# A layer norm's deviations packed by DMA ahead of the reciprocal, and three steps of the software pipeline placed anew

## The chip, the core and the metric

The kernel runs on one core of one Trainium2 chip. The metric is the device time of one execution in microseconds (us): the median of three runs of the kernel before is 827.21 us.

The engines are named as the profile does: PE (TensorE, matrix products) with PEld (its weight loads), DVE (VectorE), ACT (ScalarE), POOL (GpSimd) and SP (SyncE, which here only issues DMAs; its queue is SPq). Each runs its own instructions in order; they meet through semaphores.

## The reference

The input is x of shape (8, 64, 64, 64): 8 images, 64 channels, 64 x 64 pixels. Two layers follow each other.

Layer 0 runs four scans over the rows and then the columns of the image. Each step adds to a line the relu of a nine-tap convolution (64 to 64 channels) of the line before it: `new = cur + relu(row_conv(prev, K))`.

Layer 1 is a block of a dynamic depthwise convolution, a layer norm, and a pointwise network:

```python
pooled = x.mean((2, 3))
hdn = _ln(pooled @ w_fc1.T, ln1_w, ln1_b, axis=-1)
dyn_w = (hdn @ w_fc2.T).reshape(b * c, 1, K, K)            # K = 5, one 5x5 filter an image and channel
out = depthwise_conv(x, dyn_w)                             # padding 2
u = out.mean(1, keepdims=True)
s2 = jnp.square(out - u).mean(1, keepdims=True)
out = (out - u) * lax.rsqrt(s2 + EPS)                      # over the 64 channels of each pixel
out = ln2_w[None, :, None, None] * out + ln2_b[None, :, None, None]
out = gelu(einsum('bchw,oc->bohw', out, w_expand))         # 64 -> 256 channels, exact gelu
gx = jnp.sqrt(jnp.sum(jnp.square(out), axis=(2, 3), keepdims=True))
nx = gx / (gx.mean(1, keepdims=True) + EPS)
out = gamma * (out * nx) + beta + out
return einsum('bohw,co->bchw', out, w_shrink) + x          # 256 -> 64 channels
```

The change is about the factor `rsqrt(s2 + EPS)`, one number a pixel.

## The kernel before

`scans` computes layer 0 in the first 505 us or so; the change doesn't touch it. `block_two` computes layer 1. Two channels' halves of the image lie on the 128 partitions: partitions 0 to 63 hold the 64 channels of the even rows, 64 to 127 those of the odd rows.

**Units and slots.** The work is cut into 16 units (`UNITS`), two for each image, of 1024 columns each (`UCOLS`). The units pass through a software pipeline of slots, `for s in SLOTS_RUN`, written out by hand for each engine. In slot s

- DVE takes the taps of unit s: ten products (eleven in the units of `EARLY` = 3, 4, 5, 6, 8, 10, 12, 14), each a `scalar_tensor_tensor` into PSUM (L996), and then the addition into `inner` (`add_part`, L981). The first tap waits for PE's convolution of the unit.
- PE makes five other taps of unit s + 1 as 30 products (`conv(0)` to `conv(5)`, L1240, five products each), the statistics of unit w = s - 1 (L1255), four expansions of unit e = s - 2 (L1286) and two shrinking products of unit v = s - 5 (L1312). `conv(0)` waits for the addition into `inner` of unit s - 1.
- ACT squares unit w (L866) and the mean of it (`square_mean`, L871), takes the root (`root`, L877), and makes the four gelus of unit e (L889), squares for the energy (L899) and products for the taps of unit s + 1 (L860). Root and gelu need different activation tables, so a table load of 1.28 us stands ahead of each change.
- POOL normalises unit e (`norm`, L818: `inner` times `rstd_wide`), adds ACT's products (L793), splits x into high and low parts for PE (L783, L788) and in even slots makes the diagonals for the next image (L809).

**The way of a deviation.** `statistics` leaves mean and mean square of unit w in PSUM: in each group of 32 partitions only four rows of 128 columns are meaningful (4 groups x 4 rows x 128 = 2048 numbers, one for each pixel of the unit). `make_var` (L1030, L1032) makes the variance on DVE, ACT's `root` the deviation `std` (128 x 128, L877), `make_rstd` the reciprocal of all 128 x 128 on DVE (L1039). Then SP (`spread_rstd`, L744) stores `rstd` to DRAM (L749) and loads it back twice with a broadcast over 64 partitions each into `rstd_wide` (L756), which POOL's `norm` waits for. The last unit takes another way: PE spreads its reciprocal by products (`widen`, L1260).

**The order around the change.** DVE's order in a slot is: two taps, `finish(v, 0)`, two taps, `sum_energy` (in slots where n = s - 3 is an odd unit), `make_var`, one tap, `make_rstd`, one tap, `finish(v, 1)`, one tap (two in an `EARLY` slot), `respond` (in the same slots as `sum_energy`), and the rest of the taps with the addition. `finish` (L1090) adds the shrunk result to x. `sum_energy` and `respond` (L1065 and L1070 to L1081) turn an image's energies into the factor of the shrinking weights; PE's part of that is `respond` (L1297), which follows `conv(3)`. In the first slots there is no v, and so no `finish` (it begins in slot 5), and no n.

SP runs, slot by slot: `spread_rstd(s - 1)`, `store(s - 5)` (L742, results to DRAM) and `cross(s + 2)` (L733, L735: the other half's rows into `crossed`, after the addition of unit s).

## Time and profile before

| | before |
|---|---|
| median of three runs | 827.21 us (827.14 to 827.62) |
| the profiled execution | 827.7 us, of which the span is 826.0 us |
| PE busy | 776.0 us (94%) |
| PEld busy | 635.3 us (77%) |
| DVE busy | 624.6 us (76%) |
| POOL busy | 450.2 us (55%) |
| ACT busy | 398.9 us (48%) |

A busy share is an average over both layers. The picture in 40 slices of 20.65 us each tells the stages apart: up to slice 24 or so it is layer 0, behind that `block_two`.

```profile
## 2 busy tenths in 40 slices
PE   5999999999999999999999997978899999999886
PEld 5999998999998999999999996644445445454332
DVE  3666666666665666666888887999999999999965
ACT  5591002777774000000000003459989999999981
POOL 2333333333333333335888884988978887888610
PEclk9999999999999999999999996889999999999999
DMA  6670000000000000000000002022233334433234
```

Each digit is the busy share of a slice in tenths; PEclk is the granted clock of TensorE in tenths of full speed, DMA the mean busy share of the 16 DMA engines.

### The profile page before, as it was taken

The page shows a single profiled execution, that of the slowest core. Times are in us where ns is not written, and L with a number is a line of the kernel's source. Part 1 is how long each engine was busy: PE and PEld are TensorE (multiplying, and loading weights), DVE is VectorE, ACT ScalarE, POOL GpSimd, SP SyncE. Part 2 cuts the span into 40 slices and gives each one's busy share as a digit, 9 for nine tenths or more (in the row PEclk, how much of TensorE's full clock was granted, in tenths as well). Part 3 has the DMA queues.
Part 4 walks back from the last instruction along what each step waited for, and adds up shares of the span by engine and source line. Part 5 has one row for each costly group of instructions (what it writes and reads, how often), then busy time and mean ns, then how long its engine had stood idle before and what let it go on. Part 6 is the DMA issues. An engine that isn't in the chain of part 4 may idle for free. (4 is left out here: it accounts for less than half of the span.)

```text
span 826.0 us, 15628 instructions
## 1 busy us (share of the span) xinstructions
PE 776.0 (94%) x5399; PEld 635.3 (77%) x5399; DVE 624.6 (76%) x1143; ACT 398.9 (48%) x491; POOL 450.2 (55%) x450
## 2 busy tenths in 40 slices
PE   5999999999999999999999997978899999999886
PEld 5999998999998999999999996644445445454332
DVE  3666666666665666666888887999999999999965
ACT  5591002777774000000000003459989999999981
POOL 2333333333333333335888884988978887888610
PEclk9999999999999999999999996889999999999999
DMA  6670000000000000000000002022233334433234
GB/s 145 162 179 0 0 0 0 2 0 0 0 0 1 1 0 0 0 0 1 1 0 0 0 0 50 25 64 72 77 81 80 90 92 109 104 79 83 55 77 102
DMA packets 61571, 35.81 MB, mean 43 GB/s; under 512 B 41504, under 2 KB 59488, under 8 KB 61536
## 3 DMA queue, kind: packets, MB, share of 16 engines
q1 hardware_dynamic: 59424, 34.83, 17.8%
q10 hardware_dynamic: 2112, 0.52, 0.3%
q8 instruction: 20, 0.33, 0.2%
q14 instruction: 15, 0.12, 0.0%
HBM read 17.85 MB, written 9.37 MB: 33 GB/s over the span
## 5 line engine op out<-in xcount | busy, mean ns | idle before, releaser
L504 PE MATMUL psum<-line_hi,taps_hi 128*128 128x256 f32 x1270 | 203.0, 292 | 11.8 <-DVE taps_lo L400 8.5
L518 PE MATMUL psum<-line_lo,taps_hi 128*128 128x256 f32 x1270 | 202.5, 291 | 0.8 <-DVE line_lo L453 0.8
L512 PE MATMUL psum<-line_hi,taps_lo 128*128 128x256 f32 x1270 | 202.2, 291 | 0.0
L453 DVE SCALAR_TENSOR_TENSOR line_lo<-psum,rest 128x256 fp32r<-128x256 f32 x254 | 108.0, 425 | 123.9 <-POOL rest L285 114.9
L504 PEld LDWEIGHTS psum<-line_hi,taps_hi 128*128 128x128 f32 x1270 | 177.1, 192 | 13.0 <-issue 9.3
L518 PEld LDWEIGHTS psum<-line_lo,taps_hi 128*128 128x128 f32 x1270 | 176.4, 191 | 1.9 <-DVE line_lo L453 1.7
L512 PEld LDWEIGHTS psum<-line_hi,taps_lo 128*128 128x128 f32 x1270 | 176.9, 191 | 0.0
L285 POOL TENSOR_TENSOR rest<-x,line_hi 128x256 f32<-128x256 f32 x127 | 82.9, 652 | 168.6 <-DVE line_hi L444 168.6
L337 ACT ACTIVATE by_h<-x (+1 forms) x128 | 85.7, 669 | 106.6 <-DVE x L433 105.0
L285 POOL TENSOR_TENSOR rest<-by_h,line_hi 128x256 f32<-128x256 f32 x127 | 91.5, 720 | 83.3 <-DVE line_hi L444 83.3
L793 POOL TENSOR_TENSOR part<-part,prod 128x1008 f32<-128x1008 f32 (+2 forms) x56 | 127.5, 2276 | 17.1 <-ACT prod L860 11.3
L433 DVE TENSOR_TENSOR x<-line_hi,line_lo 128x256 f32 (+1 forms) x190 | 105.6, 556 | 0.2
L996 DVE SCALAR_TENSOR_TENSOR psum<-x,tap_all,psum 128x992 f32<-128x992 f32 (+6 forms) x88 | 103.8, 1180 | 1.4
L996 DVE SCALAR_TENSOR_TENSOR psum<-crossed,tap_cross,psum 128x1008 f32<-128x1008 f32 (+5 forms) x80 | 98.7, 1234 | 2.1 <-PE psum L1240 0.2
L1240 PE MATMUL psum<-x_hi,dyn_hi 128*128 128x512 f32 x160 | 69.0, 431 | 8.3 <-DVE inner L981 4.9
L1286 PE MATMUL psum<-normed,expand_w 64*128 64x512 f32 x224 | 65.1, 661 | 12.3 <-ACT wide L889 12.3
L444 DVE SCALAR_TENSOR_TENSOR line_hi<-psum,x 128x256 fp32r<-128x256 f32 x127 | 53.9, 424 | 22.0 <-PE psum L504 8.6
L1240 PE MATMUL psum<-x_hi,dyn_lo 128*128 128x512 f32 x160 | 68.1, 425 | 0.0
L444 DVE SCALAR_TENSOR_TENSOR line_hi<-psum,by_h 128x256 fp32r<-128x256 f32 x127 | 53.9, 425 | 17.0 <-PE psum L504 3.8
L1240 PE MATMUL psum<-x_lo,dyn_hi 128*128 128x512 f32 x160 | 65.9, 412 | 0.0
L889 ACT ACTIVATE wide<-psum,expand_bias 128x1024 f32<-128x1024 f32 x60 | 65.8, 1103 | 0.3
L293 POOL TENSOR_TENSOR line_sum<-line_sum,x 128x256 f32<-128x256 f32 x63 | 54.8, 870 | 20.2 <-DVE x L433 20.2
(159 smaller groups left out, 760.6 us busy)
## 6 DMA issues: line engine op xcount, KB each, us to landing
stage<-in_x_dram SPq DMA_DIRECT2D x32, 256.0 KB, 4.0
rstd_wide<-rstd_dram SPq DMA_DIRECT2D x30, 256.0 KB, 5.3
out_dram<-x SPq DMA_DIRECT2D x28, 256.0 KB, 5.4
crossed<-x SPq DMA_DIRECT2D x16, 256.0 KB, 3.5
crossed<-x SPq DMA_DIRECT2D x16, 240.0 KB, 3.6
rstd_dram<-rstd SPq DMA_DIRECT2D x15, 64.0 KB, 1.5
out_dram<-x ACTq DMA_DIRECT2D x4, 128.0 KB, 4.7
out_dram<-x SPq DMA_DIRECT2D x4, 128.0 KB, 4.0
```

The costliest lines, as they stand in the source:

```text
L285: pool.tensor_tensor(rest[:, slot % 2, :].rearrange("p (b i) -> p b i", b=B), x_line, line_hi[:, (slot + 1) % SLOTS, :, REACH:REACH + WP]. ...
L337: act.activation(dst, src, ACT.Copy).then_inc(turned, 1)
L433: dve.tensor_tensor(kept_line(s, row_of(s, k)), line_hi[:, made, :, part].bitcast(F32), line_lo[:, made, :, part].bitcast(F32), ALU.add).t ...
L444: dve.scalar_tensor_tensor(out=line_hi[:, (slot + 1) % SLOTS, :, part], in0=as_lines(line_ps[slot][:, 0:LINE]), scalar=0.0, in1=x_line, op ...
L453: dve.scalar_tensor_tensor(out=line_lo[:, (slot + 1) % SLOTS, :, part], in0=as_lines(line_ps[slot][:, 0:LINE]), scalar=0.0, in1=as_lines(r ...
L504: mm = pe.matmul(line_ps[slot][:, 0:LINE], taps_hi[:, s, d, :], line_hi[:, slot, :, d:d + WP], start=(d == 0), stop=(d == OFFSETS - 1))
L512: pe.matmul(line_ps[slot][:, 0:LINE], taps_lo[:, s, d, :], line_hi[:, slot, :, d:d + WP], start=False, stop=False, skip_group_check=True)
L518: mm = pe.matmul(line_ps[slot][:, 0:LINE], taps_hi[:, s, d, :], line_lo[:, slot, :, d:d + WP], start=False, stop=(d == OFFSETS - 1), skip_ ...
L793: pool.tensor_tensor(dst, dst, other, ALU.add).then_inc(part_step, 1)
L889: act.activation(grown(u)[:, m, :, c * COLS:(c + 1) * COLS], exp_set(4 * u + 2 * m + c), ACT.Gelu, bias=expand_bias[:, m:m + 1]).then_inc( ...
L996: dve.scalar_tensor_tensor(out=here, in0=src, scalar=weight, in1=here, op0=ALU.mult, op1=ALU.add).then_inc(tap_step, 1)
L1240: mm = pe.matmul(conv_ps[:, 2 * (u % 2) + c, :], weight[:, b % 2, n, :, :].rearrange("p o c -> p (o c)"), image[:, u % 2, CROWS * c:CROWS ...
```

## The change

It does three things.

1. **Packing.** Four DMAs of SP copy the meaningful rows of `std` (four partitions of 128 columns in each group of 32) into `dense`, 128 partitions of 16 columns. The reciprocal runs on `dense` and is 16 columns wide instead of 128; DVE waits for the four DMAs (`std_dense`) instead of for ACT's root. The store to DRAM takes `dense_rstd` (8 KB instead of 64), and the two loads into `rstd_wide` read the same amount from it in another arrangement. The last unit keeps the wide reciprocal.
2. **DVE's order.** Without `sum_energy` in the slot: two taps, `finish(v, 0)`, one tap, `make_var`, two taps, `finish(v, 1)`, `make_rstd`. With it: two taps, `finish(v, 0)`, two taps, `sum_energy`, `make_var`, two taps, `finish(v, 1)`, `make_rstd`. So the variance moves one tap up in half of the slots, and the reciprocal moves behind `finish(v, 1)`, and in the other half behind one tap more.
3. **PE's order.** `respond` goes ahead of `conv(3)` instead of behind it.

```diff
--- before.py
+++ after.py
@@ -600,6 +600,9 @@
         mean_sq = sb("mean_sq", [P, STAT_COLS])
         var = sb("var", [P, STAT_COLS])
         std = sb("std", [P, STAT_COLS])
+        PER = UCOLS // C
+        dense = sb("dense", [P, PER])
+        dense_rstd = sb("dense_rstd", [P, 2, PER])
         rstd = sb("rstd", [P, 2, STAT_COLS])
         rstd_wide = sb("rstd_wide", [P, UCOLS])
         normed = sb("normed", [P, UCOLS])
@@ -622,7 +625,7 @@
         tap = sb("tap", [P, B, len(PE_TAPS), 2])
         tap_hi = sb("tap_hi", [P, B, len(PE_TAPS), 2], F32R)
         tap_lo = sb("tap_lo", [P, B, len(PE_TAPS), 2], F32R)
-        rstd_dram = nc.dram_tensor("rstd_dram", [2, P, STAT_COLS], F32, kind="Internal").ap()
+        rstd_dram = nc.dram_tensor("rstd_dram", [2, P, PER], F32, kind="Internal").ap()
 
         pads = sem("pads")
         weights_mm = sem("weights_mm")
@@ -653,6 +656,7 @@
         rstd_ready = sem("rstd_ready")
         rstd_stored = [sem(f"rstd_stored{i}") for i in range(2)]
         rstd_spread = sem("rstd_spread")
+        std_dense = sem("std_dense")
         spread_made = sem("spread_made")
         wide_done = sem("wide_done")
         normed_ready = sem("normed_ready")
@@ -743,16 +747,22 @@
 
             def spread_rstd(u):
 
+                sp.wait_ge(std_ready, u + 1)
+                if u > 0:
+                    sp.wait_ge(rstd_ready, u)
+                for g in range(4):
+                    sp.dma_start(dense[32 * g:32 * g + 32, :],
+                                 std[32 * g:32 * g + 2 * SUBS, :].rearrange("q (a n) -> q a n", n=PER)).then_inc(std_dense, 16)
                 sp.wait_ge(rstd_ready, u + 1)
                 if u > 1:
                     sp.wait_ge(rstd_spread, 32 * (u - 1))
-                sp.dma_start(rstd_dram[u % 2], rstd[:, u % 2, :]).then_inc(rstd_stored[u % 2], 16)
+                sp.dma_start(rstd_dram[u % 2], dense_rstd[:, u % 2, :]).then_inc(rstd_stored[u % 2], 16)
                 sp.wait_ge(rstd_stored[u % 2], 16 * (u // 2 + 1))
                 if u > 0:
                     sp.wait_ge(normed_ready, u)
-                rows = rstd_dram[u % 2].rearrange("(g q) n -> g (q n)", g=4)
+                rows = rstd_dram[u % 2].rearrange("(g h q) n -> g h (q n)", g=4, h=2)
                 for h in range(2):
-                    mine = rows[:, SUBS * h * STAT_COLS:SUBS * (h + 1) * STAT_COLS].rearrange("(a g) n -> a g n", a=1)
+                    mine = rows[:, h, :].rearrange("(a g) n -> a g n", a=1)
                     sp.dma_start(rstd_wide[C * h:C * h + C, :].rearrange("p (g n) -> p g n", g=4),
                                  mine.to_broadcast([C, 4, SUBS * STAT_COLS])).then_inc(rstd_spread, 16)
 
@@ -1033,10 +1043,14 @@
                                          op1=ALU.min).then_inc(var_step, 1)
 
             def make_rstd(u):
-                dve.wait_ge(std_ready, u + 1)
                 if u > 1:
                     dve.wait_ge(rstd_stored[u % 2], 16 * (u // 2))
-                dve.reciprocal(rstd[:, u % 2, :], std[:, :]).then_inc(rstd_ready, 1)
+                if u < LAST:
+                    dve.wait_ge(std_dense, 64 * (u + 1))
+                    dve.reciprocal(dense_rstd[:, u % 2, :], dense[:, :]).then_inc(rstd_ready, 1)
+                else:
+                    dve.wait_ge(std_ready, u + 1)
+                    dve.reciprocal(rstd[:, u % 2, :], std[:, :]).then_inc(rstd_ready, 1)
 
             def norm(c):
                 dve.wait_ge(wide_done, c + 1)
@@ -1147,17 +1161,18 @@
                 take(2)
                 if v >= 0:
                     finish(v, 0)
-                take(2)
                 if n in range(UNITS) and n % 2 == 1:
+                    take(2)
                     sum_energy(n // 2)
+                else:
+                    take(1)
                 if w in range(UNITS):
                     make_var(w)
-                take(1)
+                take(2)
+                if v >= 0:
+                    finish(v, 1)
                 if w in range(UNITS):
                     make_rstd(w)
-                take(1)
-                if v >= 0:
-                    finish(v, 1)
                 take(1 + len(dve_taps(s)) - len(DVE_TAPS))
                 if n in range(UNITS) and n % 2 == 1:
                     respond(n // 2)
@@ -1338,9 +1353,9 @@
                 conv(1)
                 conv(2)
                 at_e(0, 1)
-                conv(3)
                 if n in range(UNITS) and n % 2 == 1:
                     respond(n // 2)
+                conv(3)
                 at_e(1, 0)
                 conv(4)
                 conv(5)
```

## Rows read from the trace of the kernel before

**Rows 1.** The waits from 640 to 783 us: engine, line, waited for, total us, times, longest.

```profile
PE psum L1286 <- ACT wide L889: 7.7, 9, 2.7
```

**Rows 2.** The windows of two slots: stretch, its length, busy time of each engine, clock, DMA.

```profile
718.70:738.20 19.50, 19.50 (x110) 9.39 (x106) 18.07 (x24) 19.11 (x21) 15.94 (x9) 1.00 0.39 93
738.20:754.30 16.10, 14.79 (x86) 7.83 (x86) 15.79 (x18) 14.44 (x17) 13.13 (x7) 1.00 0.36 91
```

**Rows 3.** The timeline of DVE, 680 to 752 us: start, duration, operation, idle time before.

```profile
701.38 1.22 DVE L981 SCALAR_TENSOR_TENSOR inner<-part,psum 128x1024 f32<-128x1024 f32 x1
...
721.34 0.75 DVE L1090 SCALAR_TENSOR_TENSOR x<-psum,out_bias,x 128x512 f32<-128x512 f32 x1 [0.18 <-PE psum L1312]
...
724.53 0.28 DVE L1030 TENSOR_TENSOR var<-psum,mean_sq 128x128 f32<-128x128 f32 x1
...
728.68 2.54 DVE L996 SCALAR_TENSOR_TENSOR psum<-x,tap_all,psum 128x992 f32<-128x992 f32 x2
732.02 0.16 DVE L1070 TENSOR_SCALAR resp<-psum 128x1 f32<-128x1 f32 x1 [0.80 <-PE psum L1297]
732.22 0.16 DVE L1072 RECIPROCAL resp<-resp 128x1 f32<-128x1 f32 x1
...
737.00 1.22 DVE L981 SCALAR_TENSOR_TENSOR inner<-part,psum 128x1024 f32<-128x1024 f32 x1
...
743.73 0.28 DVE L1030 TENSOR_TENSOR var<-psum,mean_sq 128x128 f32<-128x128 f32 x1
...
745.41 0.95 DVE L1039 RECIPROCAL rstd<-std 128x128 f32<-128x128 f32 x1
746.27 1.17 DVE L996 SCALAR_TENSOR_TENSOR psum<-x,tap_all,psum 128x992 f32<-128x992 f32 x1
...
748.01 3.65 DVE L996 SCALAR_TENSOR_TENSOR psum<-x,tap_all,psum 128x930 f32<-128x930 f32 x3
```

**Rows 4.** The timeline of ACT in the same stretch.

```profile
725.34 0.40 ACT L877 ACTIVATE std<-var,eps_col 128x128 f32<-128x128 f32 x1
...
741.50 1.28 ACT L877 ACT_TABLE_LOAD   x1
744.37 0.40 ACT L877 ACTIVATE std<-var,eps_col 128x128 f32<-128x128 f32 x1 [1.58 <-DVE var L1032]
```

**Rows 5.** The timeline of SP in the same stretch: start, time of the issue.

```profile
746.38 0.33 SPq L749 DMA_DIRECT2D rstd_dram<-rstd  x1
747.93 1.28 SPq L756 DMA_DIRECT2D rstd_wide<-rstd_dram  x2
```

**Rows 6.** The timeline of SP, 0 to 60 us: two of the small parameter loads.

```profile
22.02 0.59 SPq L252 DMA_DIRECT2D gamma<-in_L_conv_grn_gamma_dram  x1
...
23.62 0.29 SPq L256 DMA_DIRECT2D ln_wb<-in_L_conv_ln_b_dram  x1
```

**Rows 7.** The page's DMA issues: out<-in, count, KB each, median us from issue to landing.

```profile
rstd_wide<-rstd_dram SPq DMA_DIRECT2D x30, 256.0 KB, 5.3
...
crossed<-x SPq DMA_DIRECT2D x16, 256.0 KB, 3.5
...
rstd_dram<-rstd SPq DMA_DIRECT2D x15, 64.0 KB, 1.5
```

**Rows 8.** The timeline of ACT, 526 to 560 us: the squares of the mean.

```profile
534.30 0.28 ACT L871 ACTIVATE mean_sq<-psum 128x128 f32<-128x128 f32 x1 [2.99 <-PE psum L1255]
...
549.75 0.28 ACT L871 ACTIVATE mean_sq<-psum 128x128 f32<-128x128 f32 x1 [3.39 <-PE psum L1255]
```

**Rows 9.** The timeline of DVE, 526 to 645 us: the variances of slots 1 and 2.

```profile
535.19 0.28 DVE L1030 TENSOR_TENSOR var<-psum,mean_sq 128x128 f32<-128x128 f32 x1
...
550.25 0.28 DVE L1030 TENSOR_TENSOR var<-psum,mean_sq 128x128 f32<-128x128 f32 x1
```

**Rows 10.** The timeline of POOL, 526 to 752 us: two of its normalisations.

```profile
545.76 2.38 POOL L818 TENSOR_TENSOR normed<-inner,rstd_wide 128x1024 f32<-128x1024 f32 x1 [3.31 <-DMA rstd_wide<-rstd_dram]
...
719.58 2.38 POOL L818 TENSOR_TENSOR normed<-inner,rstd_wide 128x1024 f32<-128x1024 f32 x1 [3.37 <-PE psum L1286]
```

## The prediction, made before the changed kernel was built or run

> **What bounds the kernel now.** I read the page first: five engines share the second stage (from about 505 us), and from 640 us on PE, DVE and ACT are all busy nine tenths of each slice, so no share of busy time names the bound. The waits tell more: from 640 to 783 us, four pairs of slots, PE waits 7.7 us for ACT's gelu [rows 1]; ACT waits 1.58 us a pair for DVE's variance [rows 4], and DVE 0.80 us a pair for PE's response product [rows 3]. That is a ring, in which each engine waits once or twice in two slots. DVE's rows of one pair [rows 3] show its lap: the additions into `inner` at 701.38 and 737.00 give a period of 35.62 us; inside it DVE idles 0.18 us ahead of `finish` and 0.80 us ahead of `respond`, and nowhere else. The windows [rows 2] give PE 19.50 us of 19.50 in the slot with a response (I call it even) and 14.79 of 16.10 in the other (odd): PE alone needs 34.29 us for a pair. ACT [rows 4] runs without a break from its root at 725.34 to the end of the table load at 742.78 (17.44 us), then waits 1.58 us for the variance.
>
> **The gain of the small reciprocal.** A reciprocal of 128 columns takes 0.95 us and holds DVE 0.86 us from start to start; one of a single column takes 0.16 us [rows 3]. Between them lies 6.2 ns a column, so 16 columns take about 0.25 us, 0.17 from start to start. DVE saves 0.69 us in each of 15 slots (the last keeps the old form).
>
> **What the packing costs.** The reciprocal used to wait for ACT's root; now it waits for four DMAs that SP issues after the root. DVE is in order, so all later taps, the addition into `inner` and `respond` queue behind that wait; PE's next convolution and ACT's square wait for the addition. Let L be the time from the root's end to the release of DVE. No row shows such a DMA (32 partitions of 64 bytes out of 4 partitions, SBUF to SBUF). For the issue: the store of `rstd` takes 0.33 us of SP, eight rows of `ln_wb` 0.29, a column of `gamma` into 128 partitions 0.59 [rows 5, 6]. For the landing: that store, 64 KB, 1.5 us; the SBUF to SBUF load of `crossed`, 256 KB, 3.5 us [rows 7]. SP starts 0.04 us after a release and leaves as much between issues. Low end: 0.04 + 3 x 0.33 + 1.5 = 2.5 us. With slow issues: 0.04 + 3 x 0.63 + 1.5 = 3.4. With the landing of `crossed` too: 5.4 us. I take 0.37 us an issue and 1.5 for the landing, as the store of `rstd` is nearest in size: L = 0.04 + 3 x 0.41 + 1.5 = 2.8 us.
> The Trainium skill (DMA: Bandwidth & Descriptors, Anatomy of one DMA) puts most of the fixed time into the receipt of the target memory and calls HBM the heaviest; by it the landing in SBUF is under the 1.5 us of the store, which no row of this trace shows, and the sum would lean to the low end of L.
>
> **How much of L is covered.** The new place is behind two taps and `finish` after the variance. Odd slot: from the variance at 743.73 to the work after `finish` at 748.01 is 4.28 us, less the old reciprocal (746.27 - 745.41 = 0.86): 3.42 us of cover. Even slot: 728.68 - 724.53 - 0.86 = 3.29 us [rows 3]. The root ends 0.63 + 0.40 us after the variance starts (743.73 to 744.37, [rows 3, 4]) when it waits for nothing else. So the wait W is L + 0.03 + 1.03 - cover: L - 2.36 in an odd slot, L - 2.23 in an even one. At 2.8 that is 0.44 and 0.57 us, most of the 0.69 saved.
>
> **The placement.** In odd slots the variance moves one tap up (about 1.2 us) and ACT's wait of 1.58 us shrinks to nothing, since the table load ends at 742.78; the gelus come 1.2 to 1.5 us earlier and PE loses its waits (35.62 - 34.29 = 1.33 us a pair). PE's `respond` goes ahead of five products of `conv(3)`, so DVE's 0.80 us and the 0.18 go too. It moves no other queue. Costed at nothing: the rearranged order of SP. SP sits idle between `crossed` and the store, so nothing is queued behind its new waits but the chain itself.
>
> **The sum for a pair in steady state**, as the longest of three laps. PE: 34.3. DVE: 35.62 - 0.98 - 2 x 0.69 + W + W = 33.26 + 1.01 = 34.3. ACT and DVE together: root of the even slot to the end of the table load 17.44, root 0.40, L + 0.03, reciprocal 0.2, the rest of the odd slot and the even one up to its variance (748.01 to 724.53 + 35.62 is 12.14; one tap more, the 0.18 gone: 13.1), variance to root 0.63: 31.8 + L = 34.6. The last is longest: 1.0 us saved a pair. Above L = 3.15 DVE's own lap is the longest and each 0.1 us of L costs 0.2 a pair; at 2.5 PE's lap stops the gain at 1.3.
>
> **The other slots.** Slots 1 to 4 have no `finish`, so 0.65 us less cover; and in slots 1 and 2 the variance can't move up, as the mean isn't squared before 534.58 and 550.03, while DVE, a tap of 1.2 us earlier than at 535.19 and 550.25, gets there 0.6 and 1.0 us early [rows 8, 9]. Slot 1: -0.69 + 0.6 + 1.0 = +0.9. Slot 2: -0.69 + 1.0 + 1.1, less 0.2 of slack to PE, +1.2. Slot 1's reciprocal also ends 0.9 us later, and POOL's first `norm` waits for exactly that chain (3.31 us, [rows 10]); POOL then works without a break up to the operand of PE's convolution in slot 3, so the statistics of slot 3 slip and DVE gives another 0.9. Slot 4 gets back 0.4 (it has a `respond`). Together +2.6. Slots 5 to 7 have the cover of `finish`: -0.24, -0.12 and -0.24, with slack -0.7. Slots 8 to 13, three pairs: -3.1. Slots 14 and 15: -1.0. The sum at L = 2.8 is -2.2 us; the tail is unchanged. At L = 2.5 it is -5.5; at 3.0 about 0 (each 0.1 us costs some 1.1); at 3.4 it is +5.5; at 5.4 it is 2.0 us more in 15 slots, +35. The profiled execution spans 826.0 us and took 827.7, 0.5 above the median of 827.21; I take -2.2 from the median: 825.0.
>
> **The spread of `rstd`.** The reciprocal ends some 0.3 us later than before in odd slots and 1.3 in even ones. In the steady state the two loads land at 746.38 + 1.54 + 0.64 + 5.3 = 753.9, while `norm` (719.58 + 35.62 = 755.2, [rows 5, 7, 10]) waits for PE: 1.3 us of cover. After an even slot the old reciprocal ends 1.68 + 0.94 us behind the variance at 724.53, the same count gives 734.7, and what follows stands at about 737, near the addition of 737.00 [rows 3]: some 2 us of cover. Both hold, if the second only by 1 us. Were it gone, each 0.1 us would first eat the idle time of POOL, which has 3.37 us a slot there, and reach PE only behind that. The store is 8 KB instead of 64, but of as many rows; I leave it at 1.5 us.
>
> **Rivals.**
> (a) The packing is slow: SP's issues take 0.6 us each, L = 3.4 or more. For it: all back-to-back issues of wide shapes take 0.6 us [rows 6], and the two loads of `rstd_wide` 1.28 us [rows 5]; against: `ln_wb` and the store at 0.3. Place: the wait ahead of the reciprocal. It decides from L = 3.0 on, where W in 15 slots and the early slots eat all that the lap gave; at 3.4 the time is 832.7, slower. Chance 0.3 for slower in all.
> The Trainium skill (the same page, Rules for kernel authors) advises to merge many small transfers, since under 64 KB one pays mostly overhead, and says that transfers to disjoint parts of the partitions serialize. Its fixed cost of about 2.0 us a DMA, measured on GpSimd's path, is an estimate of 0.5 us more than the row: L = 3.3 and some 831. The store's 1.5 us disagrees with the figure; the direction is rival (a)'s.
> (b) The packing is quick, L at most 2.55. Then PE's lap of 34.3 is the bound and the gain stops: 821.7. Chance 0.15.
> (c) Gains and waits cancel, L from 2.9 to 3.15: 827 within 1.6. Chance 0.2.
> (d) The small reciprocal isn't small (a fixed part beyond the 0.16 us of one column). Each 0.1 us costs 0.1 in slots bound by DVE, under 1 us in all; it changes no sign and sits inside the range.
>
> **How the numbers follow.** The forecast, L from 2.55 to 2.9, has 0.35 (-4.8 to -1.7). A difference of 0.2% (1.65 us) is what a measurement of this kernel can tell from none. Faster: 0.35 + 0.15 = 0.50; same 0.20; slower 0.30. The forecast is the likeliest single case. The range runs from rival (b) (-6) to L = 3.4 (+5.3): 821.2 to 832.5; outside it are mainly landings as long as those of `crossed`.
>
> **What the profile after would show.** The reciprocal at 0.25 us; idle time of DVE ahead of it released by the DMA into `dense`, 0.4 to 0.6 us in steady slots and above 1 in slots 1 to 3: if it is zero, L is under 2.3 and (b) holds; if about 1 us or more, (a) does. Four issues of SP in 1.6 us. ACT's root no longer waiting for the variance in odd slots; `respond` on DVE without its 0.80; PE's waits for gelu gone; the period of a pair 34.6. `norm` waiting for a DMA in steady slots would show the spread too late, and I would be wrong there. I would be wrong as a whole if DVE had slack in the steady slots, so that neither W nor the 0.69 counted.

## The result, and the profile after

| | before | after |
|---|---|---|
| median | 827.17 us (827.02 to 827.62) | 841.37 us (841.01 to 841.87) |
| ratio | | 1.017, 95% interval 1.0157 to 1.0183 |
| profiled execution: span | 826.0 us | 840.1 us |
| DVE busy | 624.6 us | 616.0 us |

The changed kernel is 14 us slower, though DVE works 8.6 us less. The forecast was 825.0.

The page of the changed kernel first. Its chain of work that ended last (followed back from the last instruction, as shares of the span) says where to look: the four packing issues of SP (L754) and their landing stand on it with 7% of the span, and DVE's taps lead it.

```profile
DVE psum L1006 18%; SPq L754 4%; DMA dense<-std 3%; PE psum L1327 2%; DVE psum L1019 1%; ACT std L887 1%; DVE x L1104 1%; DVE var L1042 1%; PE psum L1270 0%; ACT dump L909 0%; DVE dense_rstd L1050 0%; DVE inner L991 0%; DVE var L1040 0%; ACT wide L899 0%; PE psum L1255 0%
```

The waits of 640 to 783 us (engine, line, waited for, total us, times, longest; before: [rows 1]): DVE's wait for `dense` is there in every slot, ACT's root waits for the variance eight times where it waited four, and PE still waits for the gelus, if less (4.7 us after 7.7).

```profile
POOL normed L828 <- DMA rstd_wide<-rstd_dram: 31.2, 8, 8.8
...
DVE dense_rstd L1050 <- DMA dense<-std: 11.7, 8, 1.5
ACT std L887 <- DVE var L1042: 8.7, 8, 1.8
...
PE psum L1301 <- ACT wide L899: 4.7, 8, 0.9
```

The windows of one pair, odd slot and even slot, from addition to addition (columns as in [rows 2]). PE is idle in both, 0.92 and 0.96 us; before, it was idle in the odd one only (1.31 us). The pair lasts 36.44 us instead of 35.62.

```profile
710.77:727.79 17.02, 16.10 (x92) 8.02 (x90) 15.27 (x17) 16.31 (x19) 13.69 (x7) 1.00 0.33 81
727.79:747.21 19.42, 18.46 (x104) 9.05 (x102) 17.41 (x24) 17.27 (x20) 15.58 (x9) 1.00 0.41 94
```

DVE's timeline of the same pair (before: [rows 3]):

```profile
716.21 0.28 DVE L1040 TENSOR_TENSOR var<-psum,mean_sq 128x128 f32<-128x128 f32 x1
...
721.32 0.25 DVE L1050 RECIPROCAL dense_rstd<-dense 128x16 f32<-128x16 f32 x1 [1.40 <-DMA dense<-std]
...
739.70 0.25 DVE L1050 RECIPROCAL dense_rstd<-dense 128x16 f32<-128x16 f32 x1 [1.52 <-DMA dense<-std]
```

ACT's roots and SP's issues in it (before: [rows 4, 5]; four issues of the packing are one row):

```profile
716.84 0.40 ACT L887 ACTIVATE std<-var,eps_col 128x128 f32<-128x128 f32 x1 [0.41 <-DVE var L1042]
...
735.22 0.40 ACT L887 ACTIVATE std<-var,eps_col 128x128 f32<-128x128 f32 x1 [1.77 <-DVE var L1042]
```

```profile
717.27 2.86 SPq L754 DMA_DIRECT2D dense<-std  x4
721.60 0.32 SPq L759 DMA_DIRECT2D rstd_dram<-dense_rstd  x1
```

DVE's part of the response (at 742.24) no longer waits, and the reciprocal costs 0.25 us, both as forecast. But from the root's end (716.84 + 0.40 = 717.24) to the reciprocal (721.32) there are 4.08 us, and again 4.08 in the even slot (735.62 to 739.70). I had taken 2.8 for this time, the L of the prediction. The four issues take 2.86 us in a row: one by one 0.72, 0.72, 0.64 and 0.64 us, a mean of 0.68, with 0.04 to 0.05 between them. The last one starts at 719.48, 2.21 us behind the first, and DVE goes on 1.84 us later.

The page's DMA issues (before: [rows 7]) show something that I had not expected: the loads of `rstd_wide` land sooner, 4.1 us after their issue instead of 5.3. (So does the results' store that follows them in the queue, 4.1 instead of 5.4.)

```profile
rstd_wide<-rstd_dram SPq DMA_DIRECT2D x30, 256.0 KB, 4.1
```

**Where the 14.1 us are.** I cut every span at the starts of the additions into `inner` (on DVE), where each slot ends. The column u1 is the time at which slot 1 ends, a pair is two slots, and the tail is all that comes behind the start of the addition of slot 15. All runs but `e13_shapes` in one table, in us of their profiled executions; the last column is the median of all executions:

| kernel | u1 | slots 2 to 5 | 6, 7 | a pair, 8 to 13 | 14, 15 | tail | span | median |
|---|---|---|---|---|---|---|---|---|
| before | 544.04 | 67.73 | 34.44 | 35.62 | 36.08 | 36.84 | 826.0 | 827.2 |
| after | 545.62 | 72.84 | 36.43 | 36.45 | 36.93 | 38.94 | 840.1 | 841.37 |
| e1_place | 544.11 | 69.14 | 34.72 | 34.72 | 35.19 | 37.78 | 825.1 | 827.82 |
| e2_pack | 546.75 | 77.21 | 39.96 | 39.99 | 40.48 | 37.72 | 862.1 | 864.02 |
| e3_free | 543.86 | 67.49 | 33.57 | 34.21 | 34.78 | 37.98 | 820.3 | 821.12 |
| e4_two | 544.36 | 71.53 | 34.35 | 34.34 | 34.80 | 38.85 | 826.9 | 827.55 |
| e12_plain | 545.50 | 71.39 | 35.70 | 35.74 | 36.22 | 38.77 | 834.8 | 836.52 |
| e9_stride | 545.83 | 73.41 | 36.36 | 36.38 | 36.85 | 38.72 | 840.3 | 842.0 |
| e5_respond | 543.97 | 67.25 | 34.45 | 34.72 | 35.20 | 37.78 | 822.8 | 823.56 |
| e15_respond | 544.60 | 66.69 | 34.46 | 34.73 | 35.18 | 36.98 | 822.1 | 823.57 |
| e6_order | 544.58 | 70.00 | 34.73 | 34.73 | 35.19 | 38.02 | 826.7 | 827.12 |
| e7_later | 542.84 | 69.18 | 33.50 | 34.21 | 34.75 | 36.99 | 819.9 | 822.07 |
| e8_tail | 543.49 | 70.70 | 34.73 | 34.73 | 35.25 | 36.75 | 825.1 | 826.91 |
| e14_after_tail | 544.96 | 73.00 | 36.43 | 36.45 | 36.98 | 37.67 | 838.4 | 841.68 |
| e10_resp_tail | 544.26 | 67.87 | 34.45 | 34.72 | 37.72 | 38.25 | 826.7 | 826.63 |
| e11_best | 543.35 | 66.25 | 33.50 | 34.26 | 35.78 | 37.13 | 818.8 | 820.98 |
| e16_best | 544.54 | 66.23 | 33.49 | 34.27 | 34.76 | 37.27 | 819.1 | 820.22 |

Of the 14.1 us by which the span grew, 6.7 arise up to slot 5 (1.6 + 5.1), 2.0 in slots 6 and 7, 2.5 in the three pairs, 0.85 in slots 14 and 15, and 2.1 in the tail. In slots 1 to 4, which have no `finish` between the variance and the reciprocal, DVE waits 2.04, 2.06, 2.19 and 2.18 us for the packing; the row is slot 3's:

```profile
573.47 0.25 DVE L1050 RECIPROCAL dense_rstd<-dense 128x16 f32<-128x16 f32 x1 [2.19 <-DMA dense<-std]
```

Each row of the table is one execution. Kernels that are the same up to slot 15 differ by 1.2 us in u1 (`e11_best`, `e16_best`) and by 1.6 in slots 2 to 5 (`e1_place`, `e8_tail`), so a difference of that size in these two columns needs a wait in the timeline beside it.

The tail, on PE (timeline, then windows: length, PE busy, granted clock, DMA share, GB/s), first of the changed kernel, then of the one before. In slot 15 PE waits 4.67 us for DVE's `finish`, where it waited 0.94, and works on at a granted clock of 0.50 and 0.70: at 0.50 it is the lower of the clock's two levels, 1.2 GHz. Eight shrinking products take 3.68 us instead of 1.94.

```profile
801.30 3.68 PE L1327 MATMUL psum<-wide,shrink_now 128*64 128x512 f32 x8 [4.67 <-DVE x L1104]
```

```profile
801.00:805.00 4.00, 3.70 (x12) 0.50 0.16 35
805.00:809.00 4.00, 4.00 (x41) 0.70 0.00 0
```

```profile
789.30 1.94 PE L1312 MATMUL psum<-wide,shrink_now 128*64 128x512 f32 x8 [0.94 <-DVE x L1090]
```

In both kernels these products start 0.14 us behind DVE's last addition (801.16 and 789.16), so the longer wait ahead of them delays nothing by itself. What delays is how long they take: the statistics of the last unit stand behind them, and DVE waits for the square of the mean 4.78 us instead of 2.72 (first the changed kernel, then the one before). These 2.06 us are all but the whole of the tail's 2.1.

```profile
807.22 0.29 DVE L1040 TENSOR_TENSOR var<-psum,mean_sq 128x128 f32<-128x128 f32 x1 [4.78 <-ACT mean_sq L881]
```

```profile
793.16 0.29 DVE L1030 TENSOR_TENSOR var<-psum,mean_sq 128x128 f32<-128x128 f32 x1 [2.72 <-ACT mean_sq L871]
```

### The profile page after: what moved, and what is told of

The parts are those of the page before. It is cut to its first block and busy times, and to the rows that moved or that the text cites. A ratio compares the mean times of both kernels' runs of the same rounds, so it can differ in the third digit from the quotient of the medians.

```text
span 840.1 us, 15702 instructions
## 1 busy us (share of the span) xinstructions
PE 777.6 (93%) x5399; PEld 634.8 (76%) x5399; DVE 616.0 (73%) x1143; ACT 399.2 (48%) x491; POOL 450.9 (54%) x450
## 5 line engine op out<-in xcount | busy, mean ns | idle before, releaser
L1301 PE MATMUL psum<-normed,expand_w 64*128 64x512 f32 x224 | 63.2, 642 | 11.6 <-ACT wide L899 11.3
```

## The experiments

**Is it the packing or the placement?** My theory after the traces was that the placement is fine and the packing's L of 4.08 us is the whole loss; the rival, that the new places of variance and response had cost something too. Three kernels take the change apart. `e1_place` is the changed kernel without the packing:

```diff
-                for g in range(4):
-                    sp.dma_start(dense[32 * g:32 * g + 32, :], ...)
-                if u < LAST:
-                    dve.wait_ge(std_dense, 64 * (u + 1))
-                    dve.reciprocal(dense_rstd[:, u % 2, :], dense[:, :])
+                dve.wait_ge(std_ready, u + 1)
+                dve.reciprocal(rstd[:, u % 2, :], std[:, :])
...
```

> The changed kernel without its packing: the reciprocal is again 128 columns wide on std itself, store and loads as before; the new places of variance, reciprocal and respond stay. Theory (the wait for the packing is the whole loss, the placement is a gain): DVE's lap of a pair falls to about 34.6 us, 824 to 825 us in all. Rival 1 (the placement costs, since variance and reciprocal come where their inputs aren't ready): 830 or more. Rival 2 (the late spread of rstd, for which POOL's norm now waits, costs): between, since the reciprocal ends late here too, about 828 to 832.

Measured: 827.82 us, 1.0003 of before (0.9994 to 1.0013). That is above the theory's 824 to 825 and just under the second rival's range. The pair is 34.72 us, 0.9 shorter than before; but slots 2 to 5 take 1.4 us more and the tail 0.9, which eats most of it. DVE's timeline of `e1_place` in the early slots shows waits for the square of the mean, in slots 2 and 3 (the rows below) and of 0.79 us in slot 5. Before, the only one of these slots' waits for it was 0.30 us in slot 3:

```profile
550.13 0.29 DVE L1030 TENSOR_TENSOR var<-psum,mean_sq 128x128 f32<-128x128 f32 x1 [1.01 <-ACT mean_sq L871]
565.99 0.29 DVE L1030 TENSOR_TENSOR var<-psum,mean_sq 128x128 f32<-128x128 f32 x1 [0.66 <-ACT mean_sq L871]
```

`e2_pack` is the packing at the old places (variance, reciprocal and response stand where the kernel before has them):

```diff
-                take(2)
-                if v >= 0:
-                    finish(v, 1)
+                take(1)
                 if w in range(UNITS):
                     make_rstd(w)
+                take(1)
+                if v >= 0:
+                    finish(v, 1)
...
```

> Packing alone, at the old places: the reciprocal stands one tap behind the variance. Cover is 1.7 us instead of 3.3 to 3.4, and the gain of the placement is gone. Theory: DVE waits about 3.4 us in each of 15 slots, a pair takes about 40 us, 860 to 866 us in all. Rival 1 (the placement costs): under 841. Rival 2 (the late spread costs): the reciprocal ends about 1.4 us earlier relative to the variance than in the changed kernel, so at or below 841.

Measured: 864.02 us, 1.0441 (1.0424 to 1.0458), as the theory had it. The waits of `e2_pack` from 640 to 783 us: DVE idles up to 3.4 us in each of the seven slots.

```profile
DVE dense_rstd L1050 <- DMA dense<-std: 23.6, 7, 3.4
```

So the packing alone costs some 36 us at the old place, and 13.5 at the new one (841.37 - 827.82). What the new place does is cover a part of L. The three steps of the placement together, without the packing, are worth nothing in all: their gain in the pairs is lost in the early slots and the tail.

`e3_free` asks what a packing that takes no time would give: the changed kernel without the four DMAs, whose reciprocal reads the first 16 columns of `std` instead.

```diff
-                    dve.wait_ge(std_dense, 64 * (u + 1))
-                    dve.reciprocal(dense_rstd[:, u % 2, :], dense[:, :])
+                    dve.wait_ge(std_ready, u + 1)
+                    dve.reciprocal(dense_rstd[:, u % 2, :], std[:, 0:PER])
...
```

> The changed kernel without the four packing DMAs and the wait for them: DVE takes the reciprocal of 16 columns of std itself (its values are therefore not those of the pixels, and the output is not the reference's). It shows what the small reciprocal and the placement give when the packing is free. Theory: 817 to 820 us, PE's lap of 34.3 us a pair is the bound. Rival 1: above 827. Rival 2: the spread comes as early as it can, so as the theory.

Measured: 821.12 us, 0.9918 (0.9902 to 0.9935), a microsecond above the forecast. In two windows that cover one pair's period (they start 2.5 and 1.3 us ahead of an addition) PE has no idle time at all:

```profile
694.93:711.93 17.00, 17.00 (x95) 8.38 (x95) 16.44 (x18) 16.87 (x19) 14.07 (x9) 1.00 0.36 88
711.93:729.22 17.29, 17.29 (x99) 8.69 (x99) 16.34 (x23) 16.85 (x20) 15.00 (x9) 1.00 0.38 92
```

The period of its pairs is 34.29 us too in slots 10 to 13 (34.04 in the pair before them). That is PE's lap as read from the kernel before [rows 2], and the end of what a change to this reciprocal can bring in a pair. The prediction's rival (b) had put that case at 821.7.

**How much of L is the number of issues?** `e4_two` leaves two of the four packing DMAs out; the other half of `dense` is set to one once.

```diff
-                for g in range(4):
+                for g in range(2):
...
```

> The changed kernel with two of the four packing DMAs (partitions 0 to 63 of dense); the other half of dense is set to one once, so the rstd of half of the pixels is wrong and the output is not the reference's. Theory: the time from the root to the release falls by two issues of 0.72 us, from 4.08 to 2.64 us, DVE waits 0.3 to 0.4 us a slot, and the time is 822 to 825 us. If the last DMA's landing and not the issues set the wait (it is queued on the DMA engines), it falls less: 830 to 836 us.

Measured: 827.55 us, 0.9997 (0.9987 to 1.0007), a miss as for the time. For the pair, 34.34 us, the theory holds: L falls by 1.35 us, to 2.73 (the root ends at 709.72), and the waits of DVE in one pair are 0.67 and 0.17 us:

```profile
712.45 0.25 DVE L1052 RECIPROCAL dense_rstd<-dense 128x16 f32<-128x16 f32 x1 [0.67 <-DMA dense<-std]
729.47 0.25 DVE L1052 RECIPROCAL dense_rstd<-dense 128x16 f32<-128x16 f32 x1 [0.17 <-DMA dense<-std]
```

What spoils the time is outside the pairs: slots 2 to 5 take 71.53 us and the tail 38.85. Slot 5 alone lasts 20.25 us (17.40 before). Late in slot 4 PE had waited 2.50 us for a gelu, and its timeline and windows show the granted clock at 0.51 right after; in slot 5 DVE then waits for PE's convolution (0.84 us) and, through ACT, for its statistics (0.79 us).

```profile
587.99 1.13 PE L1304 MATMUL psum<-normed,expand_w 64*128 64x512 f32 x4 [2.50 <-ACT wide L901]
```

```profile
590.00:596.00 6.00, 6.00 (x14) 0.51 0.43 87
```

The tail repeats that of the changed kernel: DVE's last wait for the square of the mean is 4.78 us there too. The quickest of the ten executions (825.22 us) had a mean granted clock of 0.987, the slowest (829.31) one of 0.976.

**Which part of the placement gains?** `e5_respond` and `e6_order` add one part each to the kernel before. The first has PE's response ahead of `conv(3)`:

```diff
-                conv(3)
                 if n in range(UNITS) and n % 2 == 1:
                     respond(n // 2)
+                conv(3)
```

> The kernel before with one edit: PE's respond ahead of conv(3). Theory (of the placement, only this step gains, and the variance's new place costs 3 us in slots 1, 2, 3 and 5, where the squared mean isn't ready): DVE's lap without waits is 34.7 us a pair, the addition into inner of the last unit comes 3.5 to 4.5 us earlier, and the time is 823 to 825 us, better than the 827.8 of the whole placement. Rival (PE's respond is hidden, and both steps are needed together to break the ring of waits): 826.5 or more.

Measured: 823.56 us, 0.9947 (0.9931 to 0.9964); once more as `e15_respond`, 823.57 and 0.9951 (0.9934 to 0.9968). `e6_order` has DVE's new order alone, the variance a tap earlier and the wide reciprocal behind `finish(v, 1)`:

```diff
-                take(2)
                 if n in range(UNITS) and n % 2 == 1:
+                    take(2)
                     sum_energy(n // 2)
+                else:
+                    take(1)
...
```

> The kernel before with DVE's new order alone (variance one tap up in half of the slots, wide reciprocal behind finish), respond on PE where it was. Theory: the early slots lose some 3 us while DVE waits for the squared mean, the steady pairs gain under 1 us each, 827 to 829 us. Rival (the new place of the variance is what gains): 825 or less.

Measured: 827.12 us, 0.9998 (0.9988 to 1.0007). Both theories hold. Both edits, each by itself, bring the pair to 34.7 us, and so do both together in `e1_place`: DVE's lap without idle time is the bound from there on. But DVE's order also brings the early waits for the square of the mean (slots 2 to 5: 70.00 us, against 67.25 and 66.69 with the response alone). So with the wide reciprocal DVE's new order adds nothing to the response's move and costs some 4 us beside it (827.82 against 823.56). The moves of the variance and of the reciprocal weren't taken apart.

**Can the packing be covered?** `e7_later` is the changed kernel with the reciprocal two taps later, ahead of `respond`.

```diff
                 if v >= 0:
                     finish(v, 1)
+                take(2)
                 if w in range(UNITS):
                     make_rstd(w)
-                take(1 + len(dve_taps(s)) - len(DVE_TAPS))
```

> The changed kernel with the reciprocal two taps further on, so that 5.8 us of DVE's work stand between variance and reciprocal instead of 3.4. Theory (the wait for the packing is the loss; its length of 4.08 us plus 1.06 is now covered): no wait ahead of the reciprocal from slot 5 on, pairs of 34.3 to 34.6 us, 821 to 825 us in all. Rival (the late spread of rstd, for which POOL waits, is what binds): PE then waits for the normalisation, and the time is 830 us or more.

Measured: 822.07 us, 0.9935 (0.9918 to 0.9951), as the theory had it. That is 19 us below the changed kernel, by two taps. In DVE's timeline of `e7_later` the reciprocal waits for nothing in either slot of the pair (at 709.88 and 727.11; the second is shown), with the same four issues ahead of it (2.85 us from 722.39):

```profile
727.11 0.25 DVE L1050 RECIPROCAL dense_rstd<-dense 128x16 f32<-128x16 f32 x1
```

In its windows of a pair PE is busy all the time, as in `e3_free`. POOL's `norm` waits for the loads of `rstd_wide` there too (22.4 us in eight slots), and PE feels nothing of it.

```profile
698.14:713.87 15.73, 15.73 (x90) 7.61 (x91) 15.24 (x17) 15.61 (x17) 14.02 (x7) 1.00 0.35 84
713.87:732.44 18.57, 18.57 (x105) 9.46 (x105) 17.61 (x24) 18.12 (x21) 15.14 (x9) 1.00 0.42 97
```

This settles the cause of the loss in the steady slots: it is DVE's exposed wait, not the DMAs as such, not their traffic, and not the later spread. In the early slots one thing is left: slot 3 lasted 19.98 us, with a wait of DVE of 3.91 us for the square of the mean and a granted clock of 0.82 to 0.84 on PE.

**Why does an issue take 0.68 us?** All four move 2 KB, from 4 partitions of 128 columns to 32 partitions of 16. `e12_plain` takes 32 partitions of 16 columns instead.

```diff
-                                 std[32 * g:32 * g + 2 * SUBS, :].rearrange("q (a n) -> q a n", n=PER))
+                                 std[32 * g:32 * g + 32, 0:PER])
```

> The changed kernel with each packing DMA taking 32 partitions of 16 columns of std to the 32 partitions of its group of dense, instead of 4 partitions of 128 columns: as many DMAs, as many bytes, the same queue, place and waits; the values in dense are not those that the groups need, so the part that is changed is which deviations are inverted. Theory A (the shape of the source, 4 partitions spread over 32, makes an issue on the queue of SyncE last 0.69 us): an issue falls to 0.33 to 0.40, the time from the root's end to VectorE's release from 4.08 to 2.7 to 3.0, the pair of slots from 36.44 to 34.3 to 34.8, and the time to 822 to 829. Theory B (any small DMA from SBUF to SBUF costs as much to issue): 0.69 stays, 841 within 1.5.

Measured: 836.52 us, 1.01 (1.0084 to 1.0117). SP's timeline and DVE's of `e12_plain` (its page has 1.7 us as the landing):

```profile
713.91 2.46 SPq L754 DMA_DIRECT2D dense<-std  x4
```

```profile
717.58 0.25 DVE L1050 RECIPROCAL dense_rstd<-dense 128x16 f32<-128x16 f32 x1 [1.02 <-DMA dense<-std]
```

An issue takes 0.59 us (0.62 with the gap), L is 3.7 and the time lies between the two theories, nearer to theory B: the spread shape accounts for 0.1 us an issue, and the other 0.59 are paid by the plain shape, too.

`e13_shapes` measures seven shapes in the kernel before, where nothing waits for them, once at the start of `block_two` and once in three slots:

```diff
+            for i in SHAPES:
+                shape(i, 0)
             cross(0)
...
```

> The kernel before with seven small transfers of a constant added to SyncE's queue, once at the start and once in each of three later slots, which nothing waits for: 4 partitions to 32 of SBUF (as the packing), 32 to 32 of SBUF (as the plain one), 32 to a piece of DRAM in one stretch, 64 to 64 of SBUF, 128 to one stretch of DRAM (as the store of the reciprocals after), 128 rows to DRAM with gaps between them, and 4 partitions to one stretch of DRAM. Theory A (a destination of separate rows costs the issue; one stretch is cheap): both to 32 partitions of SBUF 0.55 to 0.75 us, 64 partitions and the DRAM rows with gaps as much or more, and those to one stretch of DRAM 0.25 to 0.35. Theory B (SBUF as destination costs, DRAM doesn't): the DRAM rows with gaps are as cheap as one stretch, 0.33. Theory C (a source of few partitions costs): the two with 4 partitions 0.6 to 0.7, all others 0.3 to 0.4.

It took 828.16 us, from one execution. The timeline of SP in `e13_shapes` at 503 us, ahead of all other traffic of the stage (start, time of the issue):

```profile
503.29 0.81 SPq L776 DMA_DIRECT2D one_sbuf<-ident  x1
504.15 0.61 SPq L776 DMA_DIRECT2D even_sbuf<-ident  x1
504.80 0.59 SPq L776 DMA_DIRECT2D even_dram<-ident  x1
505.44 0.54 SPq L776 DMA_DIRECT2D all_sbuf<-ident  x1
506.02 0.58 SPq L776 DMA_DIRECT2D all_dram<-ident  x1
506.65 0.43 SPq L776 DMA_DIRECT2D gap_dram<-ident  x1
507.12 0.33 SPq L776 DMA_DIRECT2D one_low<-ident  x1
```

The packing's shape (`one_sbuf`) is the dearest here, 0.81 us, and takes 0.75 to 1.01 in the three slots, where other work of the queue is near (there one issue of `all_sbuf` even took 1.78). From 32 partitions, SBUF or DRAM as destination makes no difference (0.61 and 0.59): theory B falls. The same 2 KB from 4 partitions to one stretch of DRAM cost 0.33: the 4 partitions of the source are not dear by themselves, and theory C falls. Theory A falls too, since 32 and 128 partitions to one stretch of DRAM take 0.59 and 0.58, and rows with gaps only 0.43. None of my three orders the prices. What stands is narrower: four transfers of equal bytes were issued in 0.33 to 0.81 us, so bytes don't set the price. What does is open. The store of `dense_rstd`, in bytes and rows like `all_dram`, took 0.32 in the changed kernel, which speaks against any rule by shape alone.

**Does the compact region in DRAM land sooner, and does it matter?** `e9_stride` lays the four groups of the stored reciprocals 16 KB apart, as in the kernel before, instead of 2 KB.

```diff
-        rstd_dram = nc.dram_tensor("rstd_dram", [2, P, PER], F32, kind="Internal").ap()
+        rstd_dram = nc.dram_tensor("rstd_dram", [2, 4, 32 * STAT_COLS], ...).ap()[:, :, 0:32 * PER]
...
```

> The changed kernel with the four groups of rstd_dram 16 KB apart in DRAM instead of 2 KB. It asks why the broadcast back from rstd_dram lands in 4.1 us in the changed kernel and in 5.3 in the one before, and whether that matters. Theory A (the compact region in DRAM is what is read back faster): the landing of rstd_wide returns to about 5.3 us, and since the waits of the steady pair end elsewhere, the time stays at 841 within 2 us. Theory B (the layout has nothing to do with it, only what else is in the queues at that moment): the landing stays at 4.1, and the time at 841.

The page of `e9_stride`:

```profile
rstd_wide<-rstd_dram SPq DMA_DIRECT2D x30, 256.0 KB, 5.4
```

Theory A holds: the landing is back at 5.4 us, that of the results' store behind it at 5.5, and the time, from one execution, is 842.0. The store of the reciprocals to the spaced groups also took 0.56 us to issue where it took 0.32. The later spread isn't what bounds the changed kernel: 1.3 us on its landing move the span by 0.2.

**Is PE's wait in the last slot the tail's loss?** In slot 15 DVE reaches the `finish` that PE waits for late. Three kernels put it two taps earlier, on `e1_place` (`e8_tail`), on `e5_respond` (`e10_resp_tail`), and on the changed kernel (`e14_after_tail`).

```diff
-                    take(len(DVE_TAPS) - taken[0])
+                    take(len(DVE_TAPS) - 2 - taken[0])
                     finish(LAST - 4, 0)
```

> The placement without packing (e1_place), and in the last slot DVE's finish(11, 0) two taps earlier. Theory of the tail: PE waits 3.7 us for that finish, its granted clock then falls to half, the shrinking products and the statistics of the last unit run late. With the earlier finish PE has less idle time, the clock may hold, and the time is 825.5 to 827 us, 1 to 2 below e1_place. If the clock falls anyway in the idle time ahead of the statistics, no gain: 827.8.

> The kernel before with two edits: the response ahead of conv(3) (823.56 by itself), and in the last slot the finish that TensorE waits for two taps earlier. Theory A (the last slot's wait on VectorE costs about 1 us by TensorE's idle time and the clock after it, and this adds to the response's gain): 822.5, between 821.8 and 823.2. Theory B (the tail ends by another chain in this kernel): 823.6 within 0.4.

> The changed kernel with the last slot's finish that TensorE waits for two taps earlier. Theory A (the wait of 4.67 us and the clock of 0.50 and 0.70 behind it are what made the tail 2.1 us longer): TensorE waits 2.2 us or less there, and the time falls from 841.4 by 1 to 3, to 838.4 to 840.4. Theory B (the clock falls anyway or elsewhere in the tail): 841.4 within 0.8, or above it.

Measured: 826.91 (0.9996, 0.9986 to 1.0005) beside 827.82; 826.63 (0.9984, 0.9974 to 0.9993) beside 823.56; 841.68 (1.0171, 1.0154 to 1.0188) beside 841.37. The first lies in its forecast, but can't be told from `e1_place`; the second lies 2.6 us above both of its theories; the third is theory B.

The edit doesn't take PE's idle time away, it moves it. In `e14_after_tail` PE waits 2.10 us instead of 4.67 for the `finish`, but then 2.02 us for ACT's squares of the last unit, which come behind DVE's last addition as before:

```profile
798.25 2.82 PE L1327 MATMUL psum<-wide,shrink_now 128*64 128x512 f32 x8 [2.10 <-DVE x L1104]
803.10 1.08 PE L1270 MATMUL psum<-inner,pick 128*32 128x128 f32 x16 [2.02 <-ACT squares L876]
```

In `e8_tail` the two waits are 1.12 and 2.91 us, in `e1_place` there was one of 3.69. What the edit can save is the shrinking products between the addition and the statistics. The profiled tails are 1.3 us shorter in `e14_after_tail` and 1.0 in `e8_tail`, and DVE's last wait for the square of the mean goes from 4.78 to 3.39 and from 3.66 to 2.73 us with them.

But the medians don't follow. In the profiled execution of `e8_tail`, slot 5 lasts 20.05 us where `e1_place` has 18.51, with PE's granted clock at 0.57 from 590 to 595 us. Up to slot 15 the two kernels are the same, so this loss is not the edit's, and it hides the gain of the tail.

The windows of PE of `e10_resp_tail`, 778 to 794 us (the two with the lowest clock), show where time went in its profiled execution, which at 828.47 us is 1.8 above its median: the granted clock falls twice, the first time ahead of the place that the edit touches, where `e15_respond` shows 1.00 throughout.

```profile
778.00:782.00 4.00, 2.39 (x6) 0.74 0.08 24
...
790.00:794.00 4.00, 3.19 (x36) 0.52 0.00 0
```

Here the edit also does harm. DVE reaches the `finish` two taps earlier, finds PE's products late, and waits 2.38 us for them, with the last addition behind it:

```profile
785.16 0.75 DVE L1090 SCALAR_TENSOR_TENSOR x<-psum,out_bias,x 128x512 f32<-128x512 f32 x1 [2.38 <-PE psum L1312]
```

`e15_respond` has no such wait, and `e11_best` has one of 0.87 us. How much of the 3 us is this wait and how much the clock was not measured apart.

When the clock falls is not a matter of the kernel alone. `e5_respond` and `e15_respond` are one kernel, and in both PE waits 2.44 us for the same `finish`. In the first the eight products behind the wait take 2.64 us and the tail 37.78, in the second 1.94 and 36.98:

```profile
785.16 2.64 PE L1312 MATMUL psum<-wide,shrink_now 128*64 128x512 f32 x8 [2.44 <-DVE x L1090]
```

```profile
785.26 1.94 PE L1312 MATMUL psum<-wide,shrink_now 128*64 128x512 f32 x8 [2.44 <-DVE x L1090]
```

So the tail's loss in the changed kernel is the low clock behind PE's wait: it is measured where it acts (3.68 us for 1.94). That an edit removes it is not shown, and what decides whether the clock falls stays open. `e10_resp_tail` ranges from 824.64 to 829.03 us; its quickest execution had a mean granted clock of 0.984 and its slowest 0.976, though two others at 0.984 took 826.5 us.

**The findings together.** `e11_best` packs from unit 4 on alone, keeps the old order in slots 1 to 4, puts the reciprocal two taps behind `finish`, moves the variance only in odd slots from 7 on, and has the response ahead of `conv(3)` and the earlier last `finish`. `e16_best` is the same without the last.

```diff
+                late = w in range(PACKED, LAST)
+                answer = n in range(UNITS) and n % 2 == 1
+                take(1 if late and not answer and s >= 7 else 2)
...
+                    take(2)
+                    if v >= 0:
+                        finish(v, 1)
+                    take(2)
+                    make_rstd(w)
...
```

> What the runs so far point to, together: packing from unit 4 on alone, the variance a tap earlier only in odd slots from 7 on, the reciprocal two taps behind the finish so that the packing is covered, the response ahead of conv(3), and the last slot's finish two taps earlier. Theory A (the losses of the early slots and of the last slot are separate from the steady pair, whose bound is TensorE's 34.3): 817 to 819.5. Theory B (the early slots' losses come from TensorE's clock after idle times and move to other slots): 820 to 823, no better than the changed kernel with the reciprocal two taps later, 822.07.

> The kernel of e11_best (820.98) without its earlier finish in the last slot. If that edit loses by TensorE's clock as in e10_resp_tail, 818 to 820; if it gains as in e8_tail, 821.5 to 822.5.

Measured: 820.98 us, 0.9923 (0.9906 to 0.9940), and 820.22 us, 0.9910 (0.9894 to 0.9927), which is the fastest here, 7 us below the kernel before. The response's move alone gives 4 of them (`e15_respond`, 0.9951); the other 3 are what the covered packing and the order around it add. The second is 0.2 above the first of its two forecasts. The first lies in the range of its theory B (820 to 823), though a microsecond below `e7_later`: the early slots fell to 66.25 us as I wanted (69.18 in `e7_later`), but u1 came later by 0.5 us (within what one execution differs from another), and slots 14 and 15 took a microsecond more, of which 0.87 us are DVE's wait at the moved `finish`.

> The kernel of e5_respond once more: the kernel before with the response ahead of conv(3). It gave 0.9947 of the kernel before, 823.56. If the same kernel with the earlier finish in the last slot (0.9984, 826.63) lost by that edit, this run gives 0.994 to 0.996 again; if the two differ only by the chip and the moment, it gives 0.997 to 0.999.

This run gave 0.9951, so the gain of the response alone is not a matter of the chip or the moment, and the 3 us that `e10_resp_tail` lacks belong to its own executions.

## Why the prediction was wrong, point by point

- **L, the failed step.** The sum for L, 0.04 + 3 x 0.41 + 1.5 = 2.8 us, was too small by a third. Measured: 0.03 + 2.21 + 1.84 = 4.08. The issue was taken at 0.37 us, because the store of `rstd` seemed nearest in size, and it was 0.68 in the mean, 0.74 with the gap for the first three; the rows of [rows 6] held both 0.29 and 0.59, and size was the wrong measure of nearness (`e12_plain`, `e13_shapes`). The issues of `crossed`, the only ones from SBUF to SBUF in the kernel before, took 0.51 and 0.60 us in the median there; the sum used their landing as a bound and didn't look at their issue. That one term is 0.98 of the 1.3 us. The landing, 1.84 instead of 1.5, is the other 0.34. The stated bounds ran to 0.63 an issue, and to 3.4 us without the landing of `crossed`, so even the slow end of the range lay 0.7 us below the measured L. A price that no row shows and that is paid three times in series ahead of the last landing deserved a dear row as its center, not a cheap one.
- **From L to the time: right.** The DVE lap of 33.26 + W + W, with W = L - 2.36 and L - 2.23, gives 36.83 us a pair at L = 4.08; measured 36.45. The waits were 1.40 and 1.52 us where the formulas give 1.72 and 1.85: from the variance's start to the end of `finish` there was some 0.2 us more of DVE's work in the changed kernel than I had read from the rows of the one before, where the reciprocal stood between the two taps. At L = 2.73 (`e4_two`) DVE's own lap is 34.1 by the formula and the pair took 34.34, PE's lap; the prediction's third lap, 31.8 + L = 34.5, was 0.2 too long. At 3.7 (`e12_plain`) it says 36.07 and 35.74 was measured. `e2_pack` and `e7_later` show the other term, the cover: with one tap and no `finish` the wait is 3.4 us, with two taps more than in the changed kernel it is gone. Rival (a), with a chance of 0.3, had the mechanism, the place and the sign of what happened; its size at L = 4.08 would have been +5.5 + 6.8 x 1.5 = +15.7, against 12.0 up to the tail. So the stated mechanism was right and the forecast of a gain hung on one term. Two slips in the prediction's arithmetic change nothing: the low end of L leaves out three gaps of 0.04 us, and the 1.68 us for the even slot's reciprocal are the odd slot's (1.62 in the even one).
- **The small reciprocal: right.** 0.25 us, 0.17 from start to start. Rival (d) is out.
- **PE's lap of 34.3: right.** It is the bound in `e3_free` and `e7_later`.
- **The placement in steady slots: right, but one edit was enough.** The response's move and DVE's new order each take the ring's waits away, down to DVE's lap (34.7 us); together they gave no more than either (`e5_respond`, `e6_order`, `e1_place`). The odd slot's wait of ACT (1.58 us) turned into one of 1.77 in the even slot, behind DVE's exposed waits.
- **The early slots: the mechanism right, the sum too large.** I had +2.6 for slots 1 to 4 at L = 2.8; 1.28 us more of L in four slots make it +7.7, and up to the end of slot 4 it is +5.8. DVE's waits for the square of the mean were forecast for slots 1 and 2, with 0.6 and 1.0 us; in `e6_order` they are in slots 1, 2 and 3, with 0.64, 1.02 and 0.51 us, in `e1_place` in slots 2, 3 and 5, with 1.01, 0.66 and 0.79 us. Slot 5 I had not foreseen.
- **"The tail is unchanged": wrong, by 2.1 us.** I had looked at no wait of PE in slot 15. It became 4.67 us, and the products behind it ran at a granted clock of 0.50. The clock is where the 2.1 us come from; that the wait is what lowered it is likely but not shown.
- **The later spread: right that it costs nothing.** PE doesn't feel it in `e7_later`, and 1.3 us more of landing leave the changed kernel's time alone (`e9_stride`). The prediction had said that `norm` waiting for a DMA would show the spread too late; `norm` does wait for it in every steady slot, but in `e7_later` too, where PE idles in neither slot of the pair shown. As a sign of trouble it was badly chosen: an engine with 3 us of idle time a slot waits for something in any case.
- **The Trainium skill** (DMA: Bandwidth & Descriptors, Rules for kernel authors) spoke against the change with its advice to merge small transfers. The runs agree with its direction: four issues in series made the loss, and two of them less removed it from the pair. Its fixed cost of about 2.0 us a DMA is a figure of GpSimd's path; the 1.84 us measured here on SyncE's queue come near it, where I had held the store's 1.5 against it; with it and my issues I still had L = 3.3, so it was the issues that were missing. The other sentence that I had drawn from that page (Anatomy of one DMA), that HBM's receipt is the heaviest and a landing in SBUF therefore shorter, is not borne out: 2 KB into SBUF took 1.7 us (`e12_plain`) to 1.84, 8 KB into DRAM 1.4 in the changed kernel and 64 KB 1.5 in the one before.

## What to carry to other kernels

Count the DMAs on a chain, not their bytes: here each cost the queue 0.3 to 0.8 us in series ahead of the landing, and what an engine waits for is the last one. When a step is made cheap by a detour through DMA, ask first how much work of the waiting engine stands between the request and the use: two taps (2.4 us) more of it turned a loss of 14 us into a gain of 5, some 4 of which the response's move gives alone. And take a change apart before keeping it: of three edits here one gained (the response), one was neutral in the pairs and lost in the early slots (DVE's order, beside the response and with the wide reciprocal), and one lost at the place where it was put (the packing).

## What the runs showed of the hardware that was not expected

- Transfers of 2 KB took between 0.33 and 0.81 us to issue on SyncE's queue ahead of the stage's traffic, and up to 1.01 within it; the dearest was 4 partitions of 128 columns spread over 32 partitions of SBUF. No rule by destination, partitions or gaps fits all the rows.
- A broadcast load of 256 KB from a region of DRAM whose four groups lie 2 KB apart landed in 4.1 us, from groups 16 KB apart in 5.4, and the store of other data queued behind it landed in 4.1 and 5.5 us.
- Behind waits of 1.8 to 4.7 us PE's granted clock was 0.50 to 0.74 for some microseconds in several of these kernels, in others not, and two executions of one kernel differ in it behind the same wait of 2.44 us (`e5_respond` 2.64 us for eight products, `e15_respond` 1.94). Slots with a low clock were 1.5 to 3 us longer (slot 5 of `e8_tail` and `e4_two`), and `e4_two`, whose pairs were 1.3 us shorter than before, was no faster as a whole.
